# L0 attention's MLP: both matrices as three fp32r passes instead of one fp32 matmul

## The reference, cut to what matters

```python
def _L0_attn_ref(emb, ...):                      # D = E = 128, 8 heads, batch 4 x 1024 tokens
    a  = tanh(einsum('ble,hde->blhd', emb, Wa_w) + Wa_b)
    bg = einsum('ble,hde->blhd', emb, Wb_w) + Wb_b
    hs = scan over l of  h = a * h + bg
    Dx = emb @ D_w.T + D_b
    out = _ln((einsum('blhd,hkd->blhk', hs, C_w) + C_b) * Dx[:, :, None, :], hn_g, hn_b)
    sum_heads = (Dx + einsum('h,blhd->bld', head_w, out)) / nH
    z = sum_heads @ Wout_w.T + Wout_b
    u = z + _ln(z, norm_g, norm_b)
    ffn = gelu(u @ ffn1_w.T + ffn1_b)            # 128 -> 512, exact gelu
    h_out = u + (ffn @ ffn2_w.T + ffn2_b)        # 512 -> 128
    return h_out @ proj_w.T + proj_b
```

## Time and profile before

| what | value |
|---|---|
| median of 3 runs | 1163.65 us (1159.08 to 1170.48) |
| the profiled execution's own time | 1157.41 us |
| its span | 1155.7 us |
| busy: PE / PEld / DVE / ACT / POOL | 88% / 61% / 71% / 55% / 56% |
| chain that ended last | PE 48%, POOL 19%, DVE 13%, issue 11%, ACT 6% |
| one tile of this stage in the middle | 41.57 us |

### The profile page before, as it was taken

One profiled execution on the slowest core, in us unless ns is written; L12 is line 12 of the kernel. 1 busy time (PEld: TensorE's weight loads), 2 busy tenths in 40 slices (PEclk: granted clock), 3 DMA queues, 4 the chain that ended last, 5 costly groups with the idle time before them and its releaser, 6 DMA issues.

```text
span 1155.7 us, 16233 instructions
## 1 busy us (share of the span) xinstructions
PE 1012.9 (88%) x4744; PEld 708.9 (61%) x4744; DVE 818.6 (71%) x2327; ACT 639.3 (55%) x1265; POOL 643.6 (56%) x751
## 2 busy tenths in 40 slices
PE   6788999998979999999978989899976668989996
PEld 5335777765647667667746447777834445656663
DVE  7775886758878787888674775676744678777661
ACT  2335667765565676666543336676744345455543
POOL 4006556447998888877661026555256767663440
PEclk9899999999999999999997899999987889999998
DMA  8577767740000000000002025687710000000000
GB/s 264 193 254 250 226 213 237 255 125 24 17 12 13 14 15 12 15 5 2 1 1 67 7 71 196 214 258 225 218 50 23 24 19 28 14 24 10 10 15 23
DMA packets 63495, 105.26 MB, mean 91 GB/s; under 512 B 7888, under 2 KB 42192, under 8 KB 63376
## 3 DMA queue, kind: packets, MB, share of 16 engines
q1 hardware_dynamic: 54320, 85.60, 22.8%
q0 software_dynamic: 9088, 18.63, 5.6%
HBM read 79.29 MB, written 26.87 MB: 92 GB/s over the span
## 4 chain that ended last, share of the span: by engine, by line
PE 48%; POOL 19%; DVE 13%; issue 11%; ACT 6%; DMA 1%; another core or an unknown queue 1%; POOLq 0%; SPq 0%; ACTq 0%; DVEq 0%
PE bank L208 6%; POOL wr L678 3%; PE bank L457 3%; PE bank L455 3%; PE bank L474 3%; POOL head_rstd L1379 3%; PE bank L456 3%; PE bank L453 3%; PE bank L472 3%; PE bank L473 3%; PE bank L1193 2%; PE bank L1153 2%; PE bank L1159 2%; POOL got L678 2%; PE bank L1199 2%
## 5 line engine op out<-in xcount | busy, mean ns | idle before, releaser
L622 POOL DMA_INDIRECT spare_all<-xs,list_row x156 | 158.0, 1013 | 237.0 <-DVE list_row L786 109.8
L858 DVE TENSOR_TENSOR hid_lo<-hid,hid_hi 128x512 fp32r<-128x512 f32 (+1 forms) x184 | 112.1, 611 | 74.1 <-ACT hid L559 44.7
L558 ACT ACTIVATE hid_hi<-bank,b_up_of 128x512 fp32r<-128x512 f32 (+1 forms) x138 | 86.7, 628 | 56.0 <-PE bank L457 36.8
L559 ACT ACTIVATE hid<-bank,b_up_of 128x512 f32<-128x512 f32 (+1 forms) x184 | 113.0, 624 | 5.0 <-issue 1.7
L678 POOL DMA_INDIRECT got<-ys,y_slots x80 | 85.9, 1074 | 44.6 <-DMA ys<-spare_all 26.0
L1272 ACT ACTIVATE gate_b<-bank,head_rstd 128x128 f32<-128x128 f32 x256 | 73.1, 370 | 63.5 <-POOL head_rstd L1379 63.0
L208 PEld LDWEIGHTS bank<-ident,spare_all 128*128 128x128 f32 x476 | 61.2, 151 | 69.6 <-issue 59.2
L208 PE MATMUL bank<-ident,spare_all 128*128 128x128 f32 x476 | 78.8, 290 | 22.1 <-DVE spare_all L401 15.7
L559 ACT ACTIVATE hid<-bank,cols_sb 128x512 f32<-128x512 f32 x64 | 44.0, 687 | 91.5 <-PE bank L453 79.1
L455 PE MATMUL bank<-xh,wr 128*128 128x512 f32 (+1 forms) x184 | 78.9, 429 | 13.2 <-issue 7.0
L1379 POOL TENSOR_TENSOR head_rstd<-head_var,neg_half 128x4 f32<-128x4 f32 x64 | 75.9, 1186 | 5.3
(11 more groups left out here) (325 smaller groups left out, 2694.2 us busy)
## 6 DMA issues: line engine op xcount, KB each, us to landing
wr<-wq SPq DMA_DIRECT2D x92, 512.0 KB
wq<-wr SPq DMA_DIRECT2D x16, 512.0 KB, 5.7
ys<-spare_all SPq DMA_DIRECT2D x32, 256.0 KB
got<-in_w_mlp SPq DMA_DIRECT2D x8, 512.0 KB, 5.6
xs<-spare_all SPq DMA_DIRECT2D x16, 256.0 KB, 2.3
spare_all<-xs,list_row POOLq DMA_INDIRECT x156
out_x<-X SPq DMA_DIRECT2D x8, 256.0 KB, 2.3
ys<-in_x SPq DMA_DIRECT2D x1, 1920.0 KB
```

What stands on the lines that cost most here:

```text
L559: nc.scalar.activation(hid[:, n % HC, 0:w], bank[up_bank(n)][:, 0:w], ACT.Gelu_apprx_tanh, bias=bias).then_inc(s["gelu_done"], 1)
L622: g.indirect_dma_start(out=xin[:, j % XIN, b], out_offset=None, in_=xs, in_offset=bass.IndirectOffsetOnAxis(ap=list_row[:, n:n + 1], axis=0))\
L858: v.tensor_tensor(hid_lo[:, q, 0:w], hid[:, n % HC, 0:w], hid_hi[:, q, 0:w].bitcast(F32), ALU.subtract).then_inc(s["lo_done"], 1)
```

## The change

For tiles 0 to 6 (all but `LAST`) each chunk of both matrices is three fp32r passes: high weight x high input, low weight x high input, high weight x low input. The high part is the value rounded to fp32r, the low part what is left. The high and low parts of the two matrices are made once (ACT casts in slots 3 and 4, DVE subtracts in slots 4 and 5), in units 0, 1, 4 and 5 of `wr`. Per tile ACT writes `uT` twice (rounded and whole), DVE subtracts (`rest_of_u`, phase 7); ACT makes each gelu twice (rounded and whole), and DVE subtracts (`rest_of_gelu`, phases 0 and 1, two chunks each). The last tile keeps the fp32 matmuls.

```diff
@@ mix_pe
             def up(i, n):
-                pe.wait_ge(s["uT_ready"], i + 1)
+                if i < LAST:
+                    pe.wait_ge(s["u_lo_ready"], i + 1)
+                else:
+                    pe.wait_ge(s["uT_ready"], i + 1)
...
-                    nc.tensor.matmul(bank[7 - c % 2][:], f1[:, c * P:(c + 1) * P], uT[:], start=True, stop=True).then_inc(s["f1_in"], 1)
...
+                    nc.tensor.matmul(out[:], w[0], u_parts[0], start=True, stop=False)
+                    nc.tensor.matmul(out[:], w[1], u_parts[0], start=False, stop=False)
+                    nc.tensor.matmul(out[:], w[0], u_parts[1], start=False, stop=True).then_inc(s["f1_in"], 1)
 
             def down(i, n):
...
+                    pe.wait_ge(s["g_lo_ready"], i * HC + c + 1)
+                    nc.tensor.matmul(bank[7][:], f2_parts[0][:, c], g_hi[c], start=(c == 0), stop=False)
+                    nc.tensor.matmul(bank[7][:], f2_parts[1][:, c], g_hi[c], start=False, stop=False)
+                    ins = nc.tensor.matmul(bank[7][:], f2_parts[0][:, c], g_lo[c], start=False, stop=(c == HC - 1))
@@ mix_act
+                if i < LAST:
+                    nc.scalar.activation(u_parts[0], bank[6][:], ACT.Identity, bias=nb)
                 nc.scalar.activation(uT[:], bank[6][:], ACT.Identity, bias=nb).then_inc(s["uT_ready"], 1)
...
+                    if i < LAST:
+                        nc.scalar.activation(g_hi[c], bank[7 - c % 2][:], ACT.Gelu, bias=f1b[:, c:c + 1])
                     nc.scalar.activation(gelu_sb[:, c], bank[7 - c % 2][:], ACT.Gelu, bias=f1b[:, c:c + 1]).then_inc(s["f1_out"], 1)
...
+                if n == 3:
+                    nc.scalar.copy(f1_parts[0], f1[:]).then_inc(s["w_hi_ready"], 1)
+                if n == 4:
+                    nc.scalar.copy(f2_parts[0], f2[:]).then_inc(s["w_hi_ready"], 1)
@@ mix_dve
+            def rest_of_u(i):
+                dve.wait_ge(s["uT_ready"], i + 1)
+                v.tensor_tensor(u_parts[1], uT[:], u_parts[0].bitcast(F32), ALU.subtract).then_inc(s["u_lo_ready"], 1)
+
+            def rest_of_gelu(i, n):
+                for c in (2 * n, 2 * n + 1):
+                    dve.wait_ge(s["f1_out"], i * HC + c + 1)
+                    v.tensor_tensor(g_lo[c], gelu_sb[:, c], g_hi[c].bitcast(F32), ALU.subtract).then_inc(s["g_lo_ready"], 1)
...
                 if n < HEADS:
                     scan_head(n)
+                if phase in (0, 1) and two_before not in (None, LAST):
+                    rest_of_gelu(two_before, phase)
+                if phase == NH - 1 and before_it not in (None, LAST):
+                    rest_of_u(before_it)
                 if 0 <= n - 2 < HEADS:
                     head_stats(n - 2)
+                if n == 4:
+                    dve.wait_ge(s["w_hi_ready"], 4)
+                    v.tensor_tensor(f1_parts[1], f1[:], f1_parts[0].bitcast(F32), ALU.subtract).then_inc(s["w_lo_ready"], 1)
```

More of the change, by code:

```diff
@@ L1086, in macaron_kernel @@
         mix_sign = hid_hi[:, 7, 2 * P:3 * P]
+        LAST = TILES - 1
+        unit = wr[:].rearrange("p r h l n -> p (r h l) n")
+        f1_parts, u_parts = [unit[:, k] for k in (0, 1)], [unit[:, k] for k in (2, 3)]
+        f2_parts = [unit[:, k].rearrange("p (c e) -> p c e", c=HC) for k in (4, 5)]
+        g_hi, g_lo = [unit[:, 6 + c] for c in range(HC)], [unit[:, 10], unit[:, 11], hid_lo[:, 5], hid_lo[:, 6]]
         def mix_sems():
@@ L1092, in mix_sems @@
                 "head_rstd", "share_ready", "added", "base_in", "base_out", "z_stats", "z_rstd", "un_ready", "u_ready", "u_in", "uT_ready",
-                "f1_in", "f1_out", "f2_in", "hT_ready", "y_in", "tile_done")}
+                "f1_in", "f1_out", "f2_in", "hT_ready", "y_in", "tile_done",
+                "u_lo_ready", "g_lo_ready")}
         HEADS = NH * TILES
@@ L1192, in up @@
                         pe.wait_ge(s["f1_out"], i * HC + c - 1)
-                    nc.tensor.matmul(bank[7 - c % 2][:], f1[:, c * P:(c + 1) * P], uT[:], start=True, stop=True).then_inc(s["f1_in"], 1)
+                    out, w = bank[7 - c % 2], [blk(part, c) for part in f1_parts]
+                    if i == LAST:
+                        nc.tensor.matmul(out[:], blk(f1, c), uT[:], start=True, stop=True).then_inc(s["f1_in"], 1)
+                        continue
+                    nc.tensor.matmul(out[:], w[0], u_parts[0], start=True, stop=False)
+                    nc.tensor.matmul(out[:], w[1], u_parts[0], start=False, stop=False)
+                    nc.tensor.matmul(out[:], w[0], u_parts[1], start=False, stop=True).then_inc(s["f1_in"], 1)
             def down(i, n):
@@ L1198, in down @@
                 for c in (2 * n, 2 * n + 1):
-                    ins = nc.tensor.matmul(bank[7][:], f2[:, c], gelu_sb[:, c], start=(c == 0), stop=(c == HC - 1))
+                    if i == LAST:
+                        ins = nc.tensor.matmul(bank[7][:], f2[:, c], gelu_sb[:, c], start=(c == 0), stop=(c == HC - 1))
+                        continue
+                    pe.wait_ge(s["g_lo_ready"], i * HC + c + 1)
+                    nc.tensor.matmul(bank[7][:], f2_parts[0][:, c], g_hi[c], start=(c == 0), stop=False)
+                    nc.tensor.matmul(bank[7][:], f2_parts[1][:, c], g_hi[c], start=False, stop=False)
+                    ins = nc.tensor.matmul(bank[7][:], f2_parts[0][:, c], g_lo[c], start=False, stop=(c == HC - 1))
                 if n == 1:
@@ L1223, in mix_pe @@
                     out_of_head(n - 2)
+                if n == 2 * NH + 1:
+                    pe.wait_ge(s["w_lo_ready"], 5)
                 if phase in DOWN_AT and two_before is not None:
@@ L1227, in mix_pe @@
                     pe.wait_ge(s["rows_ready"], 1)
+                if n == NH + NH - 1:
+                    pe.wait_ge(s["w_lo_ready"], 4)
                 if phase == BASE and tile is not None:
```

3 lines of the change are left out of this document (added).

## The result

| | before | after |
|---|---|---|
| median | 1164.66 us | 1199.74 us (1197.28 to 1201.79) |
| ratio, 95% interval | | 1.0323 [1.0284, 1.0361] |
| the profiled execution's span | 1155.7 us | 1197.7 us |
| from the stage's first scan to the first `TENSOR_REDUCE` behind it | 368.6 us | 406.6 us |
| a tile in the middle (from one `u_of` to the next) | 41.5 us | 46.9 us |

The change costs 35 us between the two medians, 3.2% by the ratio of the table, where I had forecast +7 (in a range to 1181). The stage alone grew by 38.0 us in the profiled executions. The page of the changed kernel: busy times and shares, then the chain that ended last.

A forecast was written before the change was run, and what follows sets the result against it. PE was taken to bound phases 7 to 2, DVE, POOL and ACT phases 3 to 6. 4.3 - 0.2 + 2.85 + 0.3 = 7.2 us gave 1164.6 or 1170.9 on two bases; 1168 was named, range 1156 to 1181.

The forecast's parts named there:

- PE's saving: MLP chunks on PE: eight a tile, each 0.16 us less; 1.3 us a tile, 9.1 over seven tiles.
- The wait in phase 7: Phase 7: PE waits 1.0 to 1.1 us at `up` for the low part of u.
- Five subtractions at 0.65: Per tile on DVE: five subtractions of about 0.65 us each, 3.3 us in all.
- The port rival: DVE and POOL stop each other: two meetings a tile at 0.9 us, tiles 0 to 4; 1174 to 1180; chance 0.20.
- DVE's idle time takes up all but 0.4 to 1.3 us a tile: DVE's waits absorb most of the delay; a tile grows by 0.4 to 1.3 us, taken as 0.85.
- 1.55 late, absorbed in phase 2 but for 0.4: DVE is free for phase 2 about 1.55 us later; `o_of_head` of phase 3 starts about 0.4 us later.
- Size of a delay on POOL: POOL's roots of phase 3 may come 1.3 us late instead of 0.4.
- The tail: Tile 6, behind the last head: DVE late plus four subtractions, 3.35 less 0.5 slack, 2.85 us.
- the clock rival: Behind the last head: one more half-clock stretch of PE adds 2 to 4 us on top of the forecast; chance 0.05.
- where the forecast had 4.4: Stage ahead of the tail: tiles 0 to 4 4.3 us, tile 5 -0.2, subtractions of weights at the start 0.3.

The follow-up runs named there:

- e4: Changed kernel without the per-tile subtractions, the third pass reading the high part again: 1143.69 us, 0.9922 of before.
- e3: Changed kernel with the low part of u computed from PSUM (bank 6 plus bias, minus high part): 1.0302 of before.
- e9: Kernel before, with DVE taking the head's statistics twice in phases 0 and 1 (0.86 us more a slot, from PSUM): 1.0018 of before.
- e13: Kernel before, with DVE taking the head's statistics three times in phases 0 and 1 (3.4 us more a tile, from PSUM): 1.0137 of before.
- e7: Changed kernel with u's low part from PSUM ahead of `head_stats` and the four gelu subtractions behind it: 1.0128 of before.
- e12: Kernel before, with DVE instead of POOL adding the constant to a head's variance: 0.9932 of before.
- the short addition: POOL's addition of a head cut to 128 of 512 columns: kernel before with it 0.9880, changed kernel with it 1.0055 of before.
- e15: e7 with the constant of a head's variance added on DVE as in e12: 1.0151 of before.
- e5: Changed kernel with all five subtractions of a tile behind `head_stats` instead of ahead of it: 1.0336 of before.

## Why the prediction was wrong, point by point

Two steps failed: the length of the subtractions, and how much of the delay the slack takes up. The clock added to it.

**PE's saving: right.** The passes come 0.23 us apart, and without the subtractions the stage is 7.2 us shorter (e4), near the 9.1 forecast.

**The wait in phase 7: right, but for two tiles.** Forecast was 1.0 to 1.1 us. In the changed kernel it was 0.87 to 0.93 where the low part had met nothing, and 2.31 in the two tiles in which `rest_of_u` met the addition (450.10). Without that meeting these two have 1.35 (e3). The meeting cost some 1.7 us over the stage.

**Five subtractions at 0.65: this step failed.** I took the duration from a stage in which POOL makes no additions. Here the pairs of both phases 0 and 1 meet one in each of tiles 0 to 4, and `rest_of_u` in two of them, at 1.0 us each: 3.3 us of work became 5.3 or 6.4. The port rival had the mechanism, two meetings a tile and nearly their price (0.9 us), and a chance of 0.20; it had no meeting of scan and addition in phase 5, and it rested on the same small sum for the rest of the delay as the forecast, so that even its 1174 to 1180 fell short. The rows for it stood there before: POOL's additions at 426.67 and 441.10 lay across `mix_combine` in phase 7, into which the change puts one more operation of that kind, and across a scan in phase 2; in phases 0 and 1 they ran just behind the scan, where the change puts the pairs. With a POOL that adds 1.3 us in each slot of 5.3, and five more operations behind the scan, meeting had to be the forecast and not the rival. The page "SBUF — State Buffer" of the Trainium skill, section "SBUF: two separate sides", says this as a rule (whichever starts first keeps the shared pair for its whole instruction), and the trace agrees: 1.70 against 0.66 us for the subtraction that comes second, and 0.73 always for the form with a PSUM operand.

**DVE's idle time takes up all but 0.4 to 1.3 us a tile: this step failed too.** e9 shows that 1.7 us of delay in phases 0 and 1 vanish, so that "1.55 late, absorbed in phase 2 but for 0.4" was about right for such a delay. But the real one was 2.6 us of gelu subtractions and 2 of meetings, and e13 shows that 3.4 us are already beyond the slack. The step would have been too small even with the subtractions at their forecast length: in e7 the five take 3.25 us a tile, in tiles 0 to 4 none of them is held, and the tile still grows by 2.3 us and more, against 0.4 to 1.3. DVE's wait in phase 3 was still 1.41 to 1.49 us, not about 1.

**Size of a delay on POOL: too small.** I gave POOL's roots 0.4 to 1.3 us. The wait for `o_mv` rose by 28 us over the stage, 4 us a tile, and in phase 5 the order turned from "addition ahead of the scan" to "addition across the scan". In e4 the one tile in the middle with the long scan (372.05, 2.34 us) has a phase 5 of 8.28 us, the others 6.86 to 6.91: 1.4 us. Phase 5 is above 8 us in every kernel of the table with the full addition and more than e9's delay except e12, which takes work off POOL. That POOL's lateness brings this order about is argued from the times, no run sets it by itself; with the short addition phases 2 to 5 grow by the same 1.4 us (20.40 to 21.83), there with POOL and not DVE as the one that is held.

**The tail.** Forecast 2.85 us, with POOL's wide power 3 us later relative to the last head. It came 3.9 us later (from the last scan 18.94 us instead of 15.09), and the last subtractions collided too (2.34 us for two, at 639.85). From the last scan to the stage's end it is 56.6 us instead of 50.5; but in e3, with the same operations there, it is 51.7, so the 6.1 us of this one execution are 1.2 of the change and some 5 of half clock. There the granted clock stays at 0.50 from 20 to 40 us behind the last scan in the changed kernel, and falls there again from 50 us on; in e3 it is back at 1.00 some 5 us earlier and stays above 0.65. That is the clock rival, at a chance of 0.05 and 2 to 4 us: with the two slow phases 6 (2.8 us) the clock has some 8 of the 38 us. The body of the stage, from the first scan to the last, grew by 31.8 us, and that is where the forecast had 4.4.

**What stays open.** About 14 of 38 us need the long addition, about 15 of stage length go with the place of the gelus' subtractions (e3 to e7). These shares overlap, as the place decides most of the meetings, and no sum of them is claimed. What lengthens phases 4 and 5 once nothing is late in phases 0 to 2 (e7), and why e15's two gains don't add, was not settled.

## What to carry to other kernels

Before an operation with two SBUF operands is put on DVE, look on POOL's timeline for what runs in that slot: price the operation at its length plus what is left of POOL's, not at its length from another stage, or give it an operand from PSUM (0.73 us always, against 0.66 or 1.7). Look also at what POOL's operation waits for now: behind a scan that holds it up, the next place on DVE is the one in which it runs. Idle time of an engine takes up delay only to a point; where waits go around a ring of engines, find that point with a dummy operation of known length and no port conflict before counting on it. And put a new result behind what other engines wait for, unless its own consumer is waiting already (e7 against e5).

## What the runs showed of the hardware

A DVE scan of two 128x512 SBUF operands takes 1.27 us alone and 2.33 to 2.71 across a POOL addition of 1.28. The reverse holds too: POOL's small operations (128x4) take 1.03 instead of 0.23 us, and its root 1.9 instead of 1.04, when they fall behind a scan that is under way. Even a DVE operation with one small SBUF operand can be held: e12's constant, 128x4, took up to 1.63 us (median 0.17), the longest beside POOL's addition at 402.32, as this row of its timeline of DVE shows:

```profile
402.00 1.63 DVE L1457 TENSOR_SCALAR o_mv<-o_mv 128x4 f32<-128x4 f32 x1
```

The four statistics from PSUM took 0.85 to 0.89 us in all the traces, beside an addition or not. PE's passes come 0.23 us apart at the full granted clock and 0.43 in the slow stretches of phase 6, where the windows show 0.63 as the mean.
